# Last layer of a two-layer gated model on one Trainium2 core: routing entries built by matrix products, expert maps stored by expert, five experts' map loads ordered after the first gathers

## The reference

```python
x = x + tanh(g_xattn[0]) * L0_xattn(layernorm(x), ctx, ...)
x = x + tanh(g_ffn[0]) * L0_ffn(layernorm(x), ...)       # 16 experts, top 4, one shared expert
x = x + tanh(g_xattn[1]) * L1_xattn(layernorm(x), ctx, ...)
x = x + tanh(g_ffn[1]) * L1_ffn(layernorm(x), ...)

def L1_ffn(x, gate_w, W, atoms, expert_atom_weights, importance, mask_idx):   # 8 experts, top 2
    logits = clip(xt @ gate_w.T, -50, 50)
    top_w, top_idx = top_k(logits, 2)
    rw = softmax(top_w)
    deltas = softmax(expert_atom_weights) @ atoms
    weighted = deltas * sigmoid(importance)
    rows, cols = mask_idx // H, mask_idx % H
    vals = einsum('tk,tks->ts', rw, weighted[top_idx])
    contrib = segment_sum((xt[:, cols] * vals).T, rows, num_segments=H)
    return xt @ W.T + contrib.T
```

## Time and profile before

| | us |
|---|---|
| median of 3 runs | 2130.46 |
| lowest and highest run | 2130.20, 2135.11 |
| the profiled execution, its time | 2134.65 |
| the profiled execution, its span | 2132.8 |

### The profile page before, as it was taken

How to read it: one execution, slowest core, us unless ns; L and a number is a source line. 1 busy time by engine, 2 the same in 40 slices (tenths; PEclk the granted TensorE clock), 3 DMA queues, 4 the chain that set the end, 5 groups by cost and what they waited for, 6 DMA issues and landing times. The chain is left out here.

```text
span 2132.8 us, 39062 instructions
## 1 busy us (share of the span) xinstructions
PE 1850.2 (87%) x11349; PEld 1398.5 (66%) x11349; DVE 1192.3 (56%) x2716; ACT 933.3 (44%) x2661; POOL 994.7 (47%) x1046
## 2 busy tenths in 40 slices
PE   4688999999987998999999999967799998862992
PEld 1355665565556998999999999963466665521782
DVE  5566777776643875422222353328777778770445
ACT  3367676676751432322222333322566666520110
POOL 1577777787621253143333343322565544152551
PEclk9999999999978999999999999987899999985996
DMA  8678877787725597698987888644444444188647
GB/s 320 182 231 276 259 235 223 242 269 245 233 69 184 124 141 170 194 262 236 316 253 229 228 255 217 138 80 122 99 106 112 115 109 108 41 229 201 200 161 271
DMA packets 221459, 409.73 MB, mean 192 GB/s; under 512 B 53618, under 2 KB 119675, under 8 KB 214916
## 3 DMA queue, kind: packets, MB, share of 16 engines
q1 hardware_dynamic: 161804, 319.40, 49.3%
q0 software_dynamic: 31616, 62.14, 13.4%
q10 hardware_dynamic: 27840, 25.70, 5.0%
HBM read 210.46 MB, written 154.20 MB: 171 GB/s over the span
## 5 line engine op out<-in xcount | busy, mean ns | idle before, releaser
L702 ACT ACTIVATE a_P<-a_SC,a_nm 128x256 f32<-128x256 f32 x512 | 235.9, 473 | 132.0 <-DVE a_nm L604 131.2
L1212 POOL DMA_INDIRECT b_y_rows<-b_ysb,b_entry x79 | 124.5, 1575 | 335.4 <-ACT b_ysb L1359 187.1
L604 DVE TENSOR_REDUCE a_nm<-a_SC 128x2 f32<-128x512 f32 x256 | 164.8, 685 | 140.0 <-PE a_SC L835 139.8
L567 POOL TENSOR_TENSOR a_praw<-a_praw,a_phigh 128x704 f32<-128x704 f32 (+2 forms) x126 | 192.4, 1527 | 10.3
L1460 DVE TENSOR_TENSOR b_xl<-b_XT,b_xh 128x512 fp32r<-128x512 f32 x97 | 67.0, 691 | 213.4 <-ACT b_xh L1365 213.1
L846 PEld LDWEIGHTS a_T<-ident,a_P 128*128 128x128 f32 x1024 | 119.0, 144 | 83.1 <-issue 46.8
L846 PE MATMUL a_T<-ident,a_P 128*128 128x128 f32 x1024 | 147.5, 282 | 25.2 <-DVE a_PT L616 22.3
L565 POOL CAST a_phigh<-a_praw 128x704 fp32r<-128x704 f32 (+2 forms) x126 | 111.0, 881 | 99.3 <-DMA a_praw<-in_L_ffn_wd 34.6
L1466 DVE TENSOR_TENSOR b_al<-b_AT,b_ah 128x384 fp32r<-128x384 f32 x111 | 61.9, 557 | 156.7 <-ACT b_ah L1370 156.7
L2185 ACT ACTIVATE c_P<-c_SC,c_nm 128x240 f32<-128x240 f32 x256 | 115.7, 457 | 76.4 <-DVE c_P L2057 76.4
L1359 ACT ACTIVATE b_ysb<-b_Y 128x512 f32<-128x512 f32 x79 | 47.3, 599 | 224.7 <-PE b_Y L1307 222.7
(11 more groups left out here) (505 smaller groups left out, 4976.1 us busy)
## 6 DMA issues: line engine op xcount, KB each, us to landing
w_parts<-a_phigh SPq DMA_DIRECT2D x72, 352.0 KB, 3.6
w_parts<-a_praw SPq DMA_DIRECT2D x72, 352.0 KB, 4.3
b_wh<-w_parts SPq DMA_DIRECT2D x18, 1216.0 KB, 10.6
b_wl<-w_parts SPq DMA_DIRECT2D x18, 1216.0 KB, 14.6
c_q<-c_qT SPq DMA_DIRECT2D x64, 256.0 KB, 4.4
c_k<-c_kT SPq DMA_DIRECT2D x124, 128.0 KB, 2.4
b_wh<-w_parts SPq DMA_DIRECT2D x18, 704.0 KB, 5.4
b_wl<-w_parts SPq DMA_DIRECT2D x18, 704.0 KB, 7.4
```

The lines of the kernel that those rows point to most:

```text
L567: eng.tensor_tensor(raw[:, 0:k * m], raw[:, 0:k * m], r32(high[:, 0:k * m]), ALU.subtract).then_inc(plow_done, 1)
L604: eng.tensor_reduce(nm[:, g % 4, j, :], SC[j][:, :].rearrange("p (t k) -> p t k", t=BT), AX.X, ALU.max, negate=True).then_inc(topped, 1)
L702: e = eng.activation(Pr[:, i, t, :], SC[j][:, t * S:(t + 1) * S], ACT.Exp, bias=nm[:, g % 4, j, t:t + 1], accum_out=den[:, h, t:t + 1])
L1212: eng.indirect_dma_start(out=y_rows, out_offset=bass.IndirectOffsetOnAxis(ap=entry[:, r, 1:2].bitcast(U32), axis=0), in_=ysb[:, v % RING, ...
```

## The change

In `expert_ffn`, the table is turned into maps in 16 pieces of 128 rows a partition, each in two halves (512 elements a partition an instruction), worked at u = 22, 27, 33, 38 and so on to 104, each half in its own iteration, with one buffer for the piece, one for the high and one for the low part. Stores are issued three iterations after the first half, and the load of the next piece behind them. `core.maps` is now ordered by expert, so that a store is cut into pieces of 512 bytes and a map row is contiguous.

In `normed_attention`, the sums of seven of the eight batches are stored.

In `routed_maps`, logits are made with the turned tokens as the stationary side, in the order in which VectorE wants them. The two choices are found by two rounds of maximum, for twelve tiles and then for four. Counts are one accumulation. The places give a block number and a place in the block; VectorE writes both as 0/1 arrays (`in_unit`, `place`), GpSimd multiplies the first with code and weight (`picked`), and 32 products on TensorE sum them to the entries of all blocks. There is no `d_slots` any more. Maps are loaded by expert, four transfers each: expert 0 first of all, 1 and 2 after the token stores, 3 to 7 after the first four gathers have landed. Blocks 0 to 7 wait for the experts that they need, block 8 for all.

```diff
@@ expert_ffn
-    ME, MROWS = table.shape[1], 32
+    ME, MROWS, MHALF = table.shape[1], 128, 64
     MP = D // MROWS
     MAPS = KD * MP
-    NRAW, NHIGH, NLOW = 3, 4, 2
-    PIECE_AT = {u: i for i, u in enumerate([*range(2, 2 + MAPS // 2), *range(NU - MAPS // 2 - 1, NU - 1)])}
+    MFIRST = 22
+    MAP_AT = {MFIRST + (NU - 1 - MFIRST) * i // MAPS: i for i in range(MAPS)}
+    HALF_AT = {u + h: (i, h) for u, i in MAP_AT.items() for h in range(MROWS // MHALF)}
...
+            def map_high(i, h):
+                rows = slice(h * MHALF, (h + 1) * MHALF)
+                eng.wait_ge(mraw_in, 16 * (i + 1))
+                if i == 0:
+                    eng.wait_ge(rows_cleared, 32)
+                ge(eng, map_out, 32 * i)
+                eng.activation(mhigh[:, :, rows], mraw[:, rows, :].rearrange("p r e -> p e r"),
                                ACT.Copy).then_inc(mhigh_done, 1)
 
             def keep_map(i):
...
+                k, n = i // MP, slice(i % MP * MROWS, (i % MP + 1) * MROWS)
+                eng.wait_ge(mhigh_done, 2 * (i + 1))
+                eng.wait_ge(mlow_done, 2 * (i + 1))
+                for part, w in enumerate((r32(mhigh[:, :, :]), mlow[:, :, :])):
+                    eng.dma_start(core.maps[part, :, :, k, n].rearrange("e p n -> p e n"), w).then_inc(map_out, 16)
+                if i + 1 < MAPS:
+                    load_map(i + 1)
...
-                if u in PIECE_AT:
-                    map_high(PIECE_AT[u])
-                if u - 1 in PIECE_AT:
-                    keep_map(PIECE_AT[u - 1])
+                if u in HALF_AT:
+                    map_high(*HALF_AT[u])
+                if u - 3 in MAP_AT:
+                    keep_map(MAP_AT[u - 3])
@@ normed_attention
-                    if n == "O1" and b < B // 2:
+                    if n == "O1" and b < B - 1:
                         keep_sums(b)
@@ routed_maps, sync
+            def maps_of(e):
+                one = lambda part, k, n: core.maps[part, e, :, k:k + n, :]
+                eng.dma_start(r32(Mh[:, :, e, :]), one(0, 0, KD)).then_inc(maps_in[e], 16)
+                eng.dma_start(r32(Ml03[:, 0, e, :]), one(1, 0, 1).rearrange("p k n -> p (k n)")).then_inc(maps_in[e], 16)
+                eng.dma_start(r32(Ml12[:, :, e, :]), one(1, 1, 2)).then_inc(maps_in[e], 16)
+                eng.dma_start(r32(Ml03[:, 1, e, :]), one(1, 3, 1).rearrange("p k n -> p (k n)")).then_inc(maps_in[e], 16)
...
+            maps_of(0)
             for t in range(NT):
                 eng.wait_ge(xn_ready, t + 1)
-                eng.dma_start(xn_rows[t * P:(t + 1) * P, :], xn[:, t % XR, :]).then_inc(xn_kept[t % XR], 16)
-                for k in {3: (0,), 7: (1,), 11: (2, 3)}.get(t, ()):
-                    map_rows(eng, 0, k)
-            for k in (1, 2, 3):
-                map_rows(eng, 1, k)
+                eng.dma_start(xn_rows[t * P:(t + 1) * P, :], normal(t)).then_inc(xn_kept, 16)
+            for e in range(1, E):
+                if e == HELD:
+                    for r in range(AHEAD):
+                        eng.wait_ge(x_got[r % RING], 16)
+                maps_of(e)
+            for e in range(E):
+                eng.wait_ge(maps_in[e], 16 * LOADS)
+                eng.sem_inc(maps_ready, 1)
@@ routed_maps, gpsimd
-            for g in range(NG):
-                send_entries(g)
+            for k in range(K):
+                js = slice(k * NT, (k + 1) * NT)
+                eng.wait_ge(unit_known, k + 1)
+                eng.tensor_tensor(picked[:, js, :, :], in_unit[:, js, :].unsqueeze(2).to_broadcast([P, NT, 2, NR]),
+                                  code_w[:, js, :].unsqueeze(3).to_broadcast([P, NT, 2, NR]),
+                                  ALU.mult).then_inc(pick_ready, 1)
+            eng.wait_ge(xn_kept, 16 * NT)
+            eng.wait_ge(rows_known, 1)
@@ routed_maps, tensor
+            def logits(t):
+                eng.wait_ge(copied, t + 1)
+                i = int(t >= PARTS[1][0])
+                at = (t - PARTS[i][0]) * E
                 for k in range(KD):
+                    m = eng.matmul(LG[i][:, at:at + E], xT[:, t % WIDE, k, :], gwT[:, k, :],
+                                   start=(k == 0), stop=(k == KD - 1))
                 m.then_inc(lg_done, 1)
...
+            def entries():
+                for j in range(PICKS):
+                    if j % NT == 0:
+                        eng.wait_ge(pick_ready, j // NT + 1)
+                    if j % CHUNK == 0:
+                        eng.wait_ge(placed, j // CHUNK + 1)
+                    m = eng.matmul(EN[:, :], place[:, j, :], picked[:, j, :, :].rearrange("p c r -> p (c r)"),
+                                   start=(j == 0), stop=(j == PICKS - 1))
+                m.then_inc(entry_done, 1)
...
             def maps(r):
                 e = eng.value_load(plan_i[0:1, 0, r:r + 1], min_val=0, max_val=E - 1)
+                if r < FIRST_LOADED:
+                    needed = eng.value_load(plan_i[0:1, 1, r:r + 1], min_val=1, max_val=E)
+                    eng.wait_ge(maps_ready, needed)
+                if r == FIRST_LOADED:
+                    eng.wait_ge(maps_ready, E)
@@ routed_maps, vector (chosen_of: for each of two choices)
+                    eng.tensor_reduce(m[:, tiles], pt, AX.X, ALU.max).then_inc(vseq, c.inc())
+                    eng.tensor_tensor(et, pt, over(m), ALU.is_equal).then_inc(vseq, c.inc())
+                    eng.tensor_tensor(et, et, first[:, :].unsqueeze(1).to_broadcast([P, n, E]),
+                                      ALU.mult).then_inc(vseq, c.inc())
+                    eng.tensor_reduce(r1[:, tiles], et, AX.X, ALU.max).then_inc(vseq, c.inc())
+                    eng.tensor_tensor(oh[:, k, tiles, :], et, over(r1), ALU.is_equal).then_inc(vseq, c.inc())
...
+                    eng.tensor_tensor(in_unit[:, js, :], unit_of[:, :].unsqueeze(1).to_broadcast([P, NT, NR]),
+                                      at_unit[:, js].unsqueeze(2).to_broadcast([P, NT, NR]),
+                                      ALU.is_equal).then_inc(unit_known, 1)
+                for j in range(0, PICKS, CHUNK):
+                    eng.tensor_tensor(place[:, j:j + CHUNK, :],
+                                      place_of[:, :].unsqueeze(1).to_broadcast([P, CHUNK, BLOCK]),
+                                      at_place[:, j:j + CHUNK].unsqueeze(2).to_broadcast([P, CHUNK, BLOCK]),
+                                      ALU.is_equal).then_inc(placed, 1)
```

More of the change, by code:

```diff
@@ L2680, in routed_maps @@
[L2680 to L2683 removed]
+        totals = R[:, NT * E:(NT + 1) * E]
+        gw_in, maps_in, maps_ready = sem("gw_in"), [sem(f"maps_in{e}") for e in range(E)], sem("maps_ready")
+        consts, vseq = sem("consts"), sem("vseq")
@@ new lines, in routed_maps @@
+        xn_ready, xn_kept, turned, copied, lg_done = [
+            sem(n) for n in ("xn_ready", "xn_kept", "turned", "copied", "lg_done")]
+        mask_ready, counted, shifted, exped = [sem(n) for n in ("mask_ready", "counted", "shifted", "exped")]
+        unit_known, placed, pick_ready, entry_done = [
+            sem(n) for n in ("unit_known", "placed", "pick_ready", "entry_done")]
+        plan_known, rows_known = sem("plan_known"), sem("rows_known")
+        x_got = [sem(f"x_got{i}") for i in range(RING)]
@@ new lines, in count_chosen @@
+            def count_chosen(i):
+                a, b = PARTS[i]
+                eng.wait_ge(mask_ready, i + 1)
+                if i == 0:
+                    eng.wait_ge(consts, CONSTS)
+                    eng.matmul(R[:, :], ones[:, :], none[:, :], start=True, stop=False)
+                eng.matmul(R[:, a * E:b * E], earlier[:, :], mask[:, a:b, :].rearrange("p t e -> p (t e)"),
+                           start=False, stop=False)
+                for t in range(a, b):
+                    eng.matmul(R[:, (t + 1) * E:].rearrange("p (t e) -> p t e", e=E), ones[:, :],
+                               mask[:, t:t + 1, :].to_broadcast([P, NT - t, E]), start=False, stop=False)
+                if b == NT:
+                    eng.matmul(R[:, :], ones[:, :], none[:, :], start=False, stop=True).then_inc(counted, 1)
@@ L2879, in maps @@
                 eng.wait_ge(rows_low, r + 1)
                 for k in range(KD):
[L2881 removed]
+                    m = eng.matmul(y[:, :], low(r)[:, k, :], of_expert(Mh[:, k]), start=False, stop=(k == KD - 1))
                 m.then_inc(y_done, 1)
[L2884 to L2893 removed]
@@ L2894, in _ @@
-            eng.wait_ge(plan_ready, 1)
-            for i in range(2):
-                m = eng.transpose(R[0:1, i * 64:(i + 1) * 64], plan[0:64, i:i + 1], core.ident[0:64, 0:64])
-            m.then_inc(plan_turned, 1)
+            eng.wait_ge(gw_in, 16)
+            for t in range(NT + 2):
+                if t < NT:
+                    turn_tokens(t)
+                if t >= 2:
+                    logits(t - 2)
+            for i in range(len(PARTS)):
+                count_chosen(i)
+            entries()
@@ L2898, in _ @@
```

(1 more changed line is left out.)

483 lines of the change are left out of this document (181 added, 302 removed).

## The result

The changed kernel takes 2142.04 us (median of 20; 2133.99 to 2157.04), the kernel before 2135.30 (median of 20, the three shown at the head among them). The ratio is 1.0051, 95% interval 1.0035 to 1.0068: slower by half a per cent, where 1% faster was forecast and the range ended at 2130. Its executions form two groups, 11 between 2134.0 and 2142.9 and 9 between 2152.4 and 2157.0.

A forecast was written before the change was run, and what follows sets the result against it. TensorE, busy 87% of the span, was taken as the bound, except where it stands before the last layer's first product. Terms -21.4 + 1.7 - 1.0 - 8.6 + 6 + 0.5 = -22.8 us: median 2108, range 2093 to 2130.

The forecast's parts named there:

- (a): Last layer, turning tokens and logits: last logit at 1895, the middle between clock levels; some 14 us won.
- The clock rival: Last layer: token turning and logits all at low clock, second half of entries also low; +7, 2115; chance 0.20.
- (b): Last layer, last logit to first gather: scatters, landing and entry loads gone, 30.1 us; gather at 1915 against 1958.18.
- (c): Last layer: first product waits for SyncE's 20 map loads behind four gathers, 18.5 us; product at 1942.6, 21.4 earlier.
- (d): Last layer's blocks: DMA shared with maps and sums, +1.7 us (0.5 to 8); contiguous map rows, -1.0.
- (e): First expert layer: wait at 809 gone, -8.6 us; single-buffered map pieces late beside weight-load bursts, +6 (0 to 20).
- the stop at 809: First expert layer: ScalarE's 11.86 us wait for a table piece at 809.11; its removal was to win 8.6 us.
- (f): Attention: three more 512 KB stores, a transfer behind one could be late; +0.5 us (0 to 3).
- The slower one: First expert layer: ScalarE waits on the single map buffer in every gap, not in three; 2184; chance 0.11.
- No burst effect: First expert layer: ScalarE's pieces would not stand behind SyncE's burst, three gaps free; -6, 2102; chance 0.14.

The follow-up runs named there:

- gate_wide: both_sums with the logits as in the kernel before: gate weights stationary, 512 columns of four tiles streamed, result turned back; 2100.24 us, 0.9832.
- both_sums: Changed kernel with high-part store one iteration earlier, maps of experts 3 to 7 loaded without waiting, sums' loads behind the first four gathers; 2112.26 us, 0.9883.
- k_one: Changed kernel with logits from one of four 128-row parts, so wrong routing; 19.5 us from first turned tile to last logit, for 39.8.
- count_first: Changed kernel, wait for gathers kept, but experts 0 to 2 counted as ready before it; 2139.61 us, 1.0022.
- again: The changed kernel run and profiled once more with no edit; 2147.28 us, 1.0064.
- big_pieces: Changed kernel with each map store writing 4 KB runs, 128 pieces and not 1024 of 512 bytes, making wrong maps; 2135.05 us, 0.9998.
- late_pieces: Kernel before the change, only the first half of its small map pieces starting at iteration 22, not 2; 2133.99 us, 0.9992.
- warm: gate_wide with eight unused products of 512 columns ahead of the entry products; ratio 0.9825.

## Why the prediction was wrong

**(a), the logits: the largest miss, 17.4 us, and a price taken from the wrong row.** The last logit was put 24 us behind the layer's start and came 41.7 behind. A tile costs 0.89 for the transposes and 1.57 for eight records of logits. I priced those records at 0.108 from the earlier trace rows, whose stationary side is 8 columns wide; the change makes it 128 wide, and 0.196 is near the 0.22 of a transpose in the earlier trace rows, which also loads 128 columns; the prediction had that row in the same sum. At the low clock the price is worth 11 us. The other 6 are the clock. The middle between the levels was a hope: `gate_wide` shows the wide logits of before at 1.00 from 1877 to 1900, `both_sums` the new ones at 0.50 all through. My reading of the earlier trace rows was even the wrong way about: I held the 8 columns of the old stationary side for what cost the clock at 1885.3, but those products stream 512 columns, and in `gate_wide` the same products ran at 1.00 throughout. What lowered the clock at 1885.3 in the kernel before no run isolates. TensorE had just stood for VectorE's mask:

```profile
1884.18 0.19 PE L2845 MATMUL d_R<-d_mask,d_earlier 128*128 128x32 bf16 x1 [1.93 <-DVE d_mask L2972]
```

and it stood as long before 1894.10, with the clock at 0.73 over 1894 to 1897; but behind a third such wait, at 1903.98, it stayed at 1.00. `gate_wide` has no such wait among its logits.

The clock rival named the right level for the whole part; by its own price (1.73 a tile) it still gave only 7 us.

The Trainium skill, TensorE: Matmul & The Clock Gate, Part 4, says that the full clock does not engage for transposes. The runs agree with it more than the prediction did: in `k_one`, where transposes are seven tenths of the work, the clock was 0.50 for all 19.5 us. They don't agree wholly: in `gate_wide` it was at 0.93 from 1875 to 1877, when only transposes had run in the layer.

**(b), from logits to gather: right in kind, 7.4 short.** 27.4 us for the 20 forecast, against 49.3 before. VectorE's steps up to the entry products took 12.0 (forecast 11.7). The miss is the 64 entry records: priced by their 78 columns at 0.13, they took 0.217, again nearly the time of a weight load (PEld is busy 13.72 of the 13.91 us), where overlap had left 7.3. One more price was wrong and stayed nearly hidden beside them: VectorE's four comparisons of 1024 elements took 2.20 each, not the 1.22 of the earlier trace rows. Scatters, landing and entry loads are gone as said.

**(c), the added wait: the right mechanism, and a sum helped by luck.** Forecast 27.6 us from the first gather to the first product, measured 29.3 and 28.9, with TensorE waiting on SyncE's count. Two errors inside it offset each other. The 20 issues took 21.5 us (1961.11 to 1982.59), not 18.5. The gathers landed earlier than priced: the 4.9 was read in the earlier trace rows from the first gather's issue (1958.18) to the landing of the second (issued at 1959.46, 3.60 later), and the fourth landed 7.5 us behind the first issue, not 8.7. The sentence that this is firm "at about 10 us of delay either way" held in kind: `count_first` won 10 of the 23, and block 8 waited 13.9. What the prediction did not do is follow its own number: it priced the wait at over 20 us, with no reading of what DMA does in the time before. The 0 GB/s of 1926 to 1952 show that the wait protects nothing in front of it.

**(d), blocks: right.** With contiguous rows a block took 3.23 us for 3.28, so 39 blocks are 2.0 shorter (forecast 1.0; no run isolates the rows as the reason), and the shared DMA cost 1.4 in the first profile and 5.2 in `again` (forecast 1.7, 0.5 to 8). One reading of mine was off: 2089.49 in the earlier trace rows is the last block but one, the last product starts at 2092.16, and a block before the change is 3.28, not 3.24. It entered no term of the sum, but 40.6 and not 42 us follow the last product.

**(e), the first layer: one of three places right, the mechanism wrong.** -8.6 + 6 was forecast; the layer took 13.8 longer in one profile and 1.7 in the other. The prediction put the stores of 929, 1003 and 1077 beside weight loads, and priced them as late landings of 1.5 to 3 us. The last came true (iteration 58, 9.35 us at 1080.73); behind the other two the load's issue took 3.19 and 1.41, and the longest hold, 12.01, is at iteration 52, which it did not name. What happens is that the third DMA of a piece is held in its issue while too many pieces of its queue are outstanding, and ScalarE with it, with TensorE idle (6.82 us ahead of 1044.25) and at a clock of 0.50 over 1044 to 1048. The rows for it were there: the earlier trace rows had been read as 4.2 MB outstanding in pieces of 2 KB, which is some 2050 pieces, and two stores of 512 KB in pieces of 512 bytes are 2048. The limit was carried over in bytes where it counts pieces (`big_pieces`); that it lies near 2048 is an estimate from these two cases. And the stop at 809 was not worth its 8.6: `late_pieces` gave 3 in the trace, since time won ahead of a load that is nearly late ends in a wait for it (3.24 us, and a lower clock behind).

**(f).** From the last turned tokens of the first layer to the last layer's start it is 463.4 us before and 463.1 after: the three stores cost nothing.

**The rivals.** None gave the result. The slower one had the right engine and buffer, ScalarE and the single map buffer, but as a wait in every gap that decides from 28 us in all; it came as two holds of 21 us together, and needed the missing gain of (a) beside it to make the kernel slower. "No burst effect" is refuted by the holds of 8.4 to 12.0 us just behind a weight load, against 5.1 just ahead of one. The sum of the profiled kernel against the forecast: 17.4 for (a), 7.4 for (b), 1.7 for (c), 16.4 for (e), -1.2 for (d) and -0.8 for (f) make 41, and 2150.9 is 41 above the forecast span of 2110. So the forecast failed on two steps: the price and clock of the logits' records in (a), and in (e) a wait priced at a landing where the issue itself is held.

## What to carry to other kernels

Price a product by the row that shares its stationary width when it streams few columns, and ask of every new product order whether it leaves TensorE streaming or loading: at equal busy time that was worth a factor of two in the clock. Count the pieces of the DMAs that one engine issues in a row, not their bytes, and put work between them: an issue that is held stops its engine and whoever waits for it. Before a load is made to wait, read what DMA does in the time that it gives up.

## What the runs showed of the hardware

The issue of a 128-piece load took 0.60 us with 1024 pieces of its queue just ahead and 12.01 with 2048, beside the same weight load; with 256 larger pieces ahead it took 2.11. With 2048 ahead it was 5.13 and 5.10 where the stores went out 0.19 and 0.15 us before the weight load, and 12.01, 11.41 and 8.37 where they went out 0.53, 0.36 and 0.20 us after it. So under a microsecond between two engines' queues goes with 3 to 7 us of an issue; the two groups of executions, whose medians are 15 us apart, fit it.

TensorE was busy 10.00 of 10 us at a granted clock of 0.50 with PEld 10.00 (`both_sums`), and at 1.00 with PEld 4.94 (`gate_wide`). In `again` the narrow products began at the full clock (eight records in 0.96 us for 1.71) and lost it with TensorE busy 4.00 of 4 us and then 18.00 of 18. In `warm` the clock rose while 512 columns were streamed again and again (0.88 over 1923 to 1929.8), held for the first 16 entry records (1.00) and was at 0.50 after some 40 of them.
